# A two-layer conditioned sequence model in one launch: setup inside the first block's pipeline, the token search written out, and the experts' first and last steps rearranged

## What is computed

```python
# layer 0, for each batch b (cond[b] is one row of 256)
z = rmsnorm(x) @ pre_w.T
folded = mean of z[t], z[t+1], z[t+2], z[t+3]          # clamped at the end
gfold = folded * sigmoid(harmonics @ harm_w.T + harm_b) # the gate: the same for all batches
target = cond @ style_w.T                               # one row for each batch
cos = sum(l2norm(gfold) * l2norm(target))
blend = gfold + clip(cfg) * (1 + cos) / 2 * (target - gfold)
y = rmsnorm(concat(x, blend) @ merge_w.T + merge_b)
x1 = gelu(y @ ffn_w1.T + b1) @ ffn_w2.T + ffn_b2 + x
# layer 1
h = layernorm(x1) + silu(cond) @ W_ada.T + b_ada
x2 = x1 + attention(h)                                  # 16 heads of 64, q and k normalised
gate = softmax(x2 @ Wgate.T)                            # 8 experts
for each expert: take the 512 tokens with the largest gate (of 4096),
    out[those tokens] += gate * (gelu(ln(x2) @ fc1.T + b1s) @ fc2.T + b2s)
```

## Time and profile before

| | us |
|---|---|
| median of 3 runs | 1556.12 |
| the profiled execution's time | 1554.05 |
| its span, first to last instruction | 1551.9 |
| setup region of layer 0 | 0 to 29.6 |
| search, ranks and first gather (no large product) | 1262.6 to 1341.4 |
| from the last matmul to the end | 1539.2 to 1551.9 |

### The profile page before, as it was taken

How to read it: one execution, slowest core, us unless ns; L and a number is a source line. 1 busy time by engine, 2 the same in 40 slices (tenths; PEclk the granted TensorE clock), 3 DMA queues, 4 the chain that set the end, 5 groups by cost and what they waited for, 6 DMA issues and landing times. The chain is left out here.

```text
span 1551.9 us, 31212 instructions
## 1 busy us (share of the span) xinstructions
PE 1380.8 (89%) x9672; PEld 1132.0 (73%) x9672; DVE 1019.5 (66%) x2495; ACT 959.8 (62%) x2535; POOL 783.3 (50%) x736
## 2 busy tenths in 40 slices
PE   1599999997899999999999999999999852599996
PEld 1599999996567777777777776777777642498996
DVE  2686666744566777776777777677767566565642
ACT  2266656564677777778777877877787620335452
POOL 1377666654346555645654654565455410254633
PEclk9799999999999999999999999999999975699998
DMA  7122222110022222212222221222222253167652
GB/s 233 44 64 63 68 74 61 50 47 28 21 69 82 82 82 77 82 61 76 88 82 71 86 82 62 75 88 82 76 75 82 83 184 128 39 205 234 203 161 27
DMA packets 92407, 138.89 MB, mean 89 GB/s; under 512 B 8656, under 2 KB 61824, under 8 KB 92160
## 3 DMA queue, kind: packets, MB, share of 16 engines
q1 hardware_dynamic: 83600, 126.02, 24.3%
q0 software_dynamic: 6144, 8.39, 2.9%
q10 hardware_dynamic: 2544, 3.16, 0.6%
HBM read 87.20 MB, written 50.35 MB: 89 GB/s over the span
## 5 line engine op out<-in xcount | busy, mean ns | idle before, releaser
L1249 POOL TENSOR_TENSOR prob<-prob,share_p 128x512 f32<-128x512 f32 x256 | 268.1, 1053 | 329.5 <-DVE share_p L1352 329.5
L1158 ACT ACTIVATE prob<-bank,shift 128x256 f32<-128x256 f32 x512 | 236.1, 474 | 110.0 <-DVE shift L1346 109.8
L1346 DVE TENSOR_REDUCE shift<-bank 128x2 f32<-128x512 f32 x256 | 164.7, 685 | 194.8 <-PE bank L1019 189.8
L1244 POOL TENSOR_TENSOR raw_qk<-raw_qk,rq 128x512 f32<-128x512 f32 x128 | 145.6, 1149 | 65.3 <-DVE rq L100 65.3
L147 PE MATMUL bank<-wqkv_h,rowsT_h 128*128 128x512 f32 x384 | 160.7, 418 | 4.4 <-PEq L392 3.5
L1045 PE MATMUL bank<-pT,v 128*64 128x256 f32 x1024 | 139.6, 394 | 25.3 <-ACT pT L1221 25.3
L147 PE MATMUL bank<-wqkv_h,rowsT_l 128*128 128x512 f32 x384 | 152.2, 396 | 0.0
L147 PE MATMUL bank<-wqkv_l,rowsT_h 128*128 128x512 f32 x384 | 151.7, 395 | 0.0
L1019 PE MATMUL bank<-landing 64*128 64x256 f32 x1024 | 146.3, 404 | 3.1 <-ACT prob L1158 3.1
L1032 PEld LDWEIGHTS bank<-ident,prob 128*128 128x128 f32 x1024 | 109.8, 141 | 44.5 <-issue 42.1
L1032 PE MATMUL bank<-ident,prob 128*128 128x128 f32 x1024 | 141.2, 280 | 0.6 <-POOL prob L1249 0.4
(11 more groups left out here) (286 smaller groups left out, 4044.3 us busy)
## 6 DMA issues: line engine op xcount, KB each, us to landing
ew_raw<-in_fc1s SPq DMA_DIRECT2D x32, 256.0 KB, 3.3
split_w1h<-ew_h SPq DMA_DIRECT2D x32, 256.0 KB, 2.0
split_w1l<-ew_l SPq DMA_DIRECT2D x32, 256.0 KB, 2.4
ew_raw<-in_fc2s SPq DMA_DIRECT2D x32, 256.0 KB, 3.0
split_w2h<-ew_h SPq DMA_DIRECT2D x32, 256.0 KB, 2.1
split_w2l<-ew_l SPq DMA_DIRECT2D x32, 256.0 KB, 2.5
ew_h<-split_w1h SPq DMA_DIRECT2D x8, 1024.0 KB
ew_l<-split_w1l SPq DMA_DIRECT2D x8, 1024.0 KB
```

The lines of the kernel that those rows point to most:

```text
L1158: last = nc.scalar.activation(prob[at][:, n, :], score_bank[side][:, n * T:(n + 1) * T], ACT.Exp, bias=shift[:, at, n:n + 1], scale=-1.0, ...
L1244: nc.gpsimd.tensor_tensor(part, part, rq[:, n, c * 8:(c + 1) * 8].unsqueeze(2).to_broadcast([P, 8, HD]), ALU.mult).then_inc(normed, 1)
L1249: nc.gpsimd.tensor_tensor(prob[at][:, :, :], prob[at][:, :, :], share[:, at, :].unsqueeze(2).to_broadcast([P, TT, T]), ALU.mult).then_inc( ...
L1346: nc.vector.tensor_reduce(shift[:, s % 2 * 2 + side, :], score_bank[side][:, :].rearrange("p (n m) -> p n m", n=TT), AX, ALU.min).then_inc ...
```

## The change

1. The setup region is gone. Its scratch lies in the attention's tile `landing`, and its instructions are put into steps -4 to 0 of the pipeline. SyncE loads x of batch 0 first of all. `load_attention` moves to SyncE's step 1, behind waits for all readers of the scratch. The inverse root of the target rows is one GpSimd instruction.
2. The search is written out (no loop), its sums are made in fp32r, five setup instructions are put beside its waits, and TensorE makes products that nobody reads (`idle_products`) between its sums, around the ranks and in the experts' steps -2 and -1.
3. The slot numbers are taken as integers without two casts.
4. ScalarE makes one GELU of a 128x1 tile right after the routing's exponential.
5. The four gathers of an expert count on two semaphores, so that TensorE transposes the first two chunks when they have landed; scaling, splitting and fc1 wait for each half k of the width by itself. In step -2 VectorE waits for GpSimd's `hold` before it builds the next one-hot matrices.
6. The last expert's fc2 parts c = 1 and 3 go to the free fc1 banks, and each part is weighed when it alone is done.

```diff
-        with ExitStack() as u:
-            raw = sbuf(u, "raw", [P, 5632])
...
+        space, taken = landing[:, :, :].rearrange("p i n -> p (i n)"), 0
+        raw = part(P, 5632)
...
                 load_x(0)
+                sp.dma_start(ident[:, :], a["ident"]).then_inc(tables_in, 16)
+                sp.dma_start(cols[:, :], a["cols"]).then_inc(tables_in, 16)
+                for t, src in ((cond_t, ...), (style_w, ...), (cfg, a["cfg"]), (harm, a["harm"]), (harm_w, a["harm_w"]), (harm_b, ...), (ada_w, ...)):
+                    sp.dma_start(t, src).then_inc(consts_in, 16)
                 def step(t):
+                    if at(t, 1):
+                        sp.wait_ge(lo_pool, 1)
...
+                        load_attention(sp)
...
+                    if at(t, -3):          # SyncE, behind x(1) and xT(0)
+                        ...                # merge_b, ffn_b2
+                        sp.wait_ge(row_done, 1)
+                        sp.dma_start(target_rows, trow).then_inc(row_out, 16)
+                        sp.wait_ge(row_out, 16)
+                        load_row(0)
# TensorE
+                    if at(t, -2):
+                        ada_products()
                     if live(far):
                         pre(far)
...                                        # transposes of step -3 stand here
+                    if at(t, -3):
+                        setup_products()
# ScalarE
+                    if at(t, -4):
+                        load_piece(act, 0)
+                        load_piece(act, 1)
+                    if at(t, -2):
+                        act.wait_ge(gate_sum, 1)
+                        nc.scalar.activation(gate[:, :, :], gate[:, :, :], ACT.Sigmoid).then_inc(gate_done, 1)
+                        high_part(act, 1)
+                        high_part(act, 2)
+                    if at(t, -1):
+                        high_part(act, 3)
...
+                    if at(t, -3):          # behind xnT of batch 0
+                        load_piece(act, 2)
+                        load_piece(act, 3)
+                        high_part(act, 0)
+                        act.wait_ge(consts_in, 16 * 7)
+                        nc.scalar.activation(silu_t, cond_t, ACT.Silu).then_inc(silu_done, 1)
+                        act.wait_ge(setup_done, 1)
+                        nc.scalar.activation(tsq, banks[3][0:NB, 0:D], ACT.Square, accum_out=tss).then_inc(target_sq, 1)
# GpSimd: low_part(1) at step -2, the pow of tss at step -3
# VectorE
+                    if at(t, -2):
+                        dve.wait_ge(gate_done, 1)
+                        link(nc.vector.tensor_scalar(gate[:, :, :], gate[:, :, :], 0.25, None, ALU.mult))
+                        ...                # hbias, two instructions
+                    if at(t, -1):
+                        low_part(dve, nc.vector, 2).then_inc(lo_dve, 1)
+                    if at(t, 0):
+                        low_part(dve, nc.vector, 3).then_inc(lo_dve, 1)
...
+                    if at(t, -3):          # behind padded of batch 0
+                        low_part(dve, nc.vector, 0).then_inc(lo_dve, 1)
+                        ...                # cfg, two instructions; wait target_sq; trow; tss; wait setup_done
+                        ...                # gate sums, two instructions
+                        split_fold(new)
+                        dve.wait_ge(target_root, 1)
+                        nc.vector.tensor_copy(cfg, cfg).then_inc(row_done, 1)
# experts, search
+        def idle_products(n):
+            for _ in range(n):
+                nc.tensor.matmul(banks[7][:, 0:P], ident[:, :], ident[:, :], start=True, stop=True)
-                    with pe.Fori(0, DIGITS // TURN) as i:
-                        for k in range(TURN):
-                            pe.wait_ge(counted, i * TURN + k + 1)
-                            nc.tensor.matmul(banks[1][:, 0:4], tables[:, P:2 * P], count[:, :], start=True, stop=True).then_inc(totalled, 1)
+                    idle_products(6)
+                    for n in range(DIGITS):
+                        pe.wait_ge(counted, n + 1)
+                        nc.tensor.matmul(banks[1][:, 0:4], same[:, :], count[:, :], start=True, stop=True).then_inc(totalled, 1)
+                        idle_products(6)
...                                        # 6 more before the gates, 12 at the region's end
-                    link(vec.tensor_scalar(flat(part_i), flat(slot_i), 31, None, ALU.bitwise_and))
-                    link(vec.tensor_copy(flat(low), flat(part_i)))
-                    link(vec.tensor_scalar(flat(part_i), flat(slot_i), 5, None, ALU.arith_shift_right))
-                    link(vec.tensor_copy(flat(high), flat(part_i)))
+                    vec.tensor_scalar(flat(low), flat(slot_i), 31, None, ALU.bitwise_and)
+                    link(vec.tensor_scalar(flat(high), flat(slot_i), 5, None, ALU.arith_shift_right))
# experts, pipeline, TensorE
+                    if first(later):       # step -2
+                        idle_products(12)
+                    if first(new):         # step -1
+                        idle_products(12)
...
-                        wait_e(pe, gathered, 16 * CC, new, 16 * CC)
-                        for k in range(KT):
-                            for c in range(CC):
+                        for c in range(CC):
+                            if c % 2 == 0:
+                                wait_e(pe, gathered[c // 2], 32, new, 32)
+                            for k in range(KT):
                                 last = nc.tensor.transpose(...)
+                                if c == CC - 1:
+                                    last.then_inc(tr_done, 1)
+                            if first(new):
+                                idle_products(2 if c == 1 else 8 if c == 3 else 0)
# VectorE
+                        for k in range(KT):
+                            wait_e(dve, gT_out, KT, new, k + 1)
+                            link(vec.tensor_copy(g_h[:, k, :], gT[:, k, :]))
+                            vec.tensor_tensor(g_l[:, k, :], gT[:, k, :], g_h[:, k, :].bitcast(F32), ALU.subtract).then_inc(g_split, 1)
...
+                    if first(later):
+                        dve.wait_ge(held, 2)
```

More of the change, by code:

```diff
@@ new lines, in first_block, with part @@
+        space, taken = landing[:, :, :].rearrange("p i n -> p (i n)"), 0
+        def part(rows, n):
+            nonlocal taken
+            taken += n
+            return space[0:rows, taken - n:taken]
+        raw = part(P, 5632)
+        cond_t, silu_t, style_w, ada_w = (part(P, KT * n).rearrange("p (k n) -> p k n", k=KT) for n in (NB, NB, D, D))
+        harm, harm_w, harm_b = part(16, T), part(16, D), part(P, D)
+        trow, tsq, tss, cfg = part(NB, D + 2), part(NB, D), part(NB, 1), part(NB, 1)
@@ L375, in at, with first @@
             return isinstance(t, int) and t == step
+        def first(b):
+            return isinstance(b, int) and b == 0
         def steps(eng, step, link=None, per=0):
@@ L684, in split, with split_fold @@
                     return nc.vector.tensor_tensor(lo, src, hi.bitcast(F32), ALU.subtract)
+                def split_fold(b):
+                    wait(dve, folded, 1, b, 1)
+                    wait(dve, pre_done, 1, b - 1, 1)
+                    split(fold_h[:, :, :], fold_l[:, :, :], fold[:, :, :]).then_inc(fold_split, 1)
                 def weight_low(f):
@@ L765, in step @@
                                                 ALU.add).then_inc(x1_done, 1)
-                    if live(new):
-                        wait(dve, folded, 1, new, 1)
-                        wait(dve, pre_done, 1, new - 1, 1)
-                        split(fold_h[:, :, :], fold_l[:, :, :], fold[:, :, :]).then_inc(fold_split, 1)
+                    if live(new) and not at(t, -3):
+                        split_fold(new)
                     if live(next_):
@@ L1421, in experts @@
         gate_h, gate_l = (sbuf(s, f"gate_{p}", [P, TILES, E], F32R) for p in "hl")
-        low, high = sbuf(s, "slot_low", [P, TILES, E]), sbuf(s, "slot_high", [P, TILES, E])
+        low, high = (sbuf(s, f"slot_{n}", [P, TILES, E], I32) for n in ("low", "high"))
         b1 = sbuf(s, "b1", [P, E * G2])
@@ L1515, in _ @@
                     wide = lambda t: t[:, :].unsqueeze(2).to_broadcast([P, TILES, E])
+                    vec.memset(units[:, 0:1], 0)
+                    for k in range(1, 4):
+                        vec.memset(units[:, k:k + 1], k << (2 * DIGITS - 2))
+                    link.note(vec.memset(ones[:, :], 1.0))
                     link(vec.reduce_max(peak[:, :], logit[:, :, :], AX))
@@ L1529, in _ @@
-                    vec.tensor_copy(ones_r[:, :], ones[:, :])
-                    vec.tensor_copy(spread[:, :], tables[0:32, 2 * P:3 * P])
-                    vec.memset(count[:, 0:1], float(TOKENS))
-                    vec.memset(units[:, 0:1], 0)
-                    for k in range(1, 4):
```

(20 more changed lines are left out.)

282 lines of the change are left out of this document (132 added, 150 removed).

## The result

The changed kernel takes **1516.00 us** (median, 1515.56 to 1516.99) beside 1555.84 for the kernel before on the same chip (1554.93 to 1556.91): ratio 0.975, 95% interval 0.9738 to 0.9763. The forecast was 1515 with a range of 1508 to 1526. The profiled execution took 1515.56 with a span of 1513.7, against 1554.05 and 1551.9.

What follows compares the result with a forecast made beforehand. Three serial stretches (setup with pipeline fill, search with first gather, end) were taken to bound the kernel; terms summed to 40.9 us off 1554.05, giving 1513.1, and 2.1 for the median gave 1515 us, range 1508 to 1526.

Steps and rivals of the forecast that it cites:

- setup: Start of the kernel: setup put into the pipeline's steps, 28.9 us less delays of 2.7, 2.4 and 0.5, gains 23.3 us.
- ahead of the search: Just before the search: five copies leave the path, five memsets come in front; 1.2 us gained.
- search: Fifteen digits: no loop turns (2.2 us), shorter sums (4.5), less 0.7 for copies and 0.3 for early digits; 5.7 us gained.
- masks, ranks, casts: Behind the search: mask and rank products at the high clock gain 1.05 us, two casts dropped gain 0.75.
- list: First token list: 32 products at the high clock gain 0.9 us, the product behind them 0.15.
- hold: First gather: with VectorE waiting for it, GpSimd's `hold` takes 0.2 us instead of 1.10; 0.9 us gained.
- last landing to the end of the first fc1: From the last gather's landing: 19.25 us before, end at +14.25 now, by high clock, halves and no table load; gains 5.0.
- end, with all that is left: Kernel's end: one scatter instead of two follows the last product, so the last issue begins 1.96 us earlier.
- constants: Setup: both queues' 1.76 MB land at 8 to 9 us; SyncE's 1.0 MB alone would give 6 us.
- target row: Setup: row stored and read back at 3.0 us each, there at 20.6 us; delays dot products 2.4 us, 5.1 with store 5.7.
- half hidden: Rival, 17%: setup landing times as before (store 5.7, constants at 12) and step 1's loads 3 us late; 1524 us.
- Table load: Silu and GELU: a table switch costs 1.28 us; by the skill's 2.66, up to 1.4 more gained at fc1, lost at Silu.

Runs made afterwards that it cites:

- e7: Changed kernel with w2's load moved to 16.6 us and merge's low part on GpSimd moved behind step -2's fold; 1518.66 us, ratio 0.9762 to the kernel before.
- e5: Changed kernel with w2's 1 MB load moved behind the high part of w1, asked for at 16.55 us; 1516.29 us, ratio 0.9747 to the kernel before.
- e9: Changed kernel with w2's load asked for behind the squares of batch 2's x, at 21.13 us; 1514.62 us, against 1555.56 for the kernel before.
- four corners: Four kernels' digit times between loop turns: 2.56 us before the change, 2.35 with the clock alone, 2.34 with the single fp32r sum alone, 2.24 with both.
- e2: Changed kernel with idle products kept only in the search; 1520.35 us, ratio 0.9779 to the kernel before.
- e12: Changed kernel with w2 loaded behind batch 2's x and other counts of idle products behind the search (8, 18, 6); 1515.53 us, ratio 0.9746 to the kernel before.
- e11: The changed kernel itself, measured and profiled once more; 1518.30 us, ratio 0.9764 to the kernel before.
- e1: Changed kernel without any idle products; 1522.40 us, ratio 0.9790 to the kernel before.
- e6: Changed kernel with the merge_b and ffn_b2 bias loads moved behind the target row's load; 1514.97 us in one execution, against 1556.42 for the kernel before.

## Why the prediction was right, and where it was off

| step of the sum | forecast | measured, from the table of instants |
|---|---|---|
| setup | 23.3 | 20.9 at the search (21.3 at gf of batch 3) |
| ahead of the search | 1.2 | 1.4 |
| search | 5.7 | 6.7 |
| masks, ranks, casts | 1.8 | 1.5 |
| list | 1.05 | 0.8 |
| hold | 0.9 | 0.3 |
| last landing to the end of the first fc1 | 5.0 | 4.8 |
| end, with all that is left | 1.96 | 1.9 |
| sum | 40.9 | 38.2, the difference of the spans; the rows are rounded |

That the median came within 1 us of 1515 is partly luck: 2.7 us were missing in the sum, and the profiled execution lay nearer to the median this time (0.4 us instead of 2.1).

- **Setup.** The constants came at 8.96 (8 to 9 forecast), which fits the 1.76 MB of both queues and not the 6 us by SyncE's alone. x took 3.8 us to land instead of 2.64, beside other loads: 1.2 us later. gf(0) at 19.17 (17.4 forecast): the 1.8 us are mostly `mrg_l` stopping xn(1); without that it is 17.8 (e7). I had put `mrg_l` down as hidden since GpSimd had time, and had not asked what it does to VectorE beside it. It cost nothing only because of the mis-sized term, the **target row**: I took 3.0 us for the store, it took 5.0, and the row was there at 23.1 instead of 20.6. I had looked for the old 5.7 us in SyncE's own queue; the traffic that counts was on ScalarE's queue, w2 as e5 and e9 show, and perhaps w1. That is near the 5.7 I had kept for the range, one of the three parts of the rival "half hidden". The other two did not happen: the constants were not at 12, and `load_attention`'s five issues took 7.4 us in step 1 (68.38 to 75.79), less than half of the 15.6 before, and delayed nothing.
- **Search.** The four corners bear out 0.32 us for each digit, of which the fp32r sum with the written-out code is 0.22 and the clock 0.10 (with the clock first, 0.11 and 0.21), 15 x 0.32 = 4.8, and 0.45 to 0.51 for each of four turns, 1.9. The 0.7 for copies beside the waits was not lost: the digit with the longest of them is not longer.
- **Masks and ranks** gained 0.23 us less, since the 12 idle products at the end of the region were still running when VectorE was done, and the regions part only when all engines are (e2, without them, and e12, with 8: 6.85 and 6.84).
- **Hold.** The step that failed: the wait was priced by the instruction it frees, and the next one on GpSimd met the same VectorE work.
- **First fc1.** 4.8 of 5.0, in an execution where the clock was high. With the clock fallen at the wrong moment the list-to-list time is 0.7 us (e11) to 1.5 us (e5) longer, a rival I did not have.
- **Table load.** Silu and the gate's sigmoid run right behind a 1.28 us load (10.19 + 1.28 and 11.48; 12.88 + 1.28 and 14.17), as GELU did in the earlier trace rows, so the sum by that row held, not the 2.66 us that the Trainium skill (ScalarE: Activation LUTs, "What ACT_TABLE_LOAD costs") gives.

## What to carry to other kernels

A small store or load on the critical path can be held up for 2 to 3 us by a megabyte in flight beside it, whichever queue asked for that; move the megabyte behind both the store and the reload, since moving it between them only moves the wait. When an instruction moves to GpSimd, or a wait frees one there, look at what VectorE does in the same microseconds and at the next GpSimd instruction too: of the 0.9 us freed at `hold`, 0.7 came back there. Short products that keep TensorE's clock up pay where the engine has time for them even at the low clock; in front of a product that waits for data they were 2.7 us in the way once the clock had fallen (e12).

## What the runs showed of the hardware

- TensorE's granted clock stayed at 1.00 through fifteen digits of 2.24 us with a pause of 0.52 us in each; without the short products it was 0.50 throughout (e1).
- The same program fell to 0.50 at 1295.5 in one execution and at 1303.3 in another, and was back about 3 us later in both; in e9 and e12 it took about 7.
- GpSimd's issue of a gather takes 0.96 us alone, 1.40 to 1.43 beside VectorE's 128x512 operations and 2.14 where it starts beside its 128x1024 one; VectorE's scaling takes 0.61 us alone and 2.73 beside a GpSimd subtraction of 2.40.
- The same 16 KB store landed in 4.4 to 5.2 us with two 1 MB loads asked for ahead of it (3.9 in e6, without the two bias loads), and in 1.4 to 3.2 with one. Programs that are the same up to it still differ by 0.6 to 1.0 us (5.0 and 4.4; 1.6 and 2.3; 2.2 and 3.2).
